# Attention pooling on one core: in TensorE's column-tiled stretch, the sums of the chunk before last are written ahead of the scores of the last one

## The chip, the cores and the metric

The kernel runs on one core of a Trainium2 chip. The metric is the device time of one execution in microseconds (us), lower is better. A core has five engines with instruction streams of their own that wait for each other by semaphores: TensorE (PE in the profile; PEld is its weight load), VectorE (DVE), ScalarE (ACT), GpSimd (POOL) and SyncE (SP), which here only issues DMAs.

## The reference

There are 512 rows (B), each with 200 behaviour vectors (S) of 128 numbers (E) and one candidate vector. Cut to what matters:

```python
W_b, W_c = fc1_w[:E], fc1_w[E:]
h = relu(einsum('bse,eh->bsh', behavior_emb, W_b) + (candidate_emb @ W_c)[:, None, :] + fc1_b)
scores = einsum('bsh,h->bs', h, fc2_w[:, 0]) + fc2_b[0]
attn = softmax(scores, axis=-1)
user_interest = einsum('bse,bs->be', behavior_emb, attn)
x = concatenate([user_interest, candidate_emb], axis=1)
z = relu(x @ mlp1_w + mlp1_b)
logit = (z @ mlp2_w + mlp2_b)[:, 0]
```

All inputs are float32. Nearly all the work is in the first product (512 x 200 vectors times a 128x128 matrix), in the scores and in `user_interest`.

## The kernel before, in words

**Chunks and groups.** The 512 rows are worked on in 32 chunks of 16 rows. A chunk is read twice: as `xt` (transposed, 128 x 4 groups x 800 columns, for the first product) and as `x` (128 x 3200, for the weighted sums). Each goes through four buffers. A group `g` is 800 columns of `xt`, the vectors of 4 rows.

**The first product** is made in three fp32r matmuls: ScalarE casts a group to its high half `xh` (`high_half`, L311), VectorE subtracts that from the original to give the low half `xl` (`low_half`, L440), and TensorE adds `w_hi*xh`, `w_lo*xh` and `w_hi*xl` in PSUM (`products`, L577, L578, L581). A group's result takes two banks; three such pairs (`z_ps0` to `z_ps2`) are used in turn. VectorE reads the results of groups 0 and 2 out (`biased_max`, L450) and ScalarE those of groups 1 and 3 (`biased_relu`, L355), both into `hidden`. So `products` of group 1 of a chunk waits, by `hidden_made` (`banks_read`, L568), until VectorE has read out group 2 of the chunk before it, whose banks it takes.

**Scores.** `score` (L594) multiplies `hidden` with the second layer's column, as 8 small matmuls: four column tiles of the array, one for each group, first with a 32-column weight and 416 columns, then with a 1-column weight and 384 columns. They fill the single bank `s_ps`. VectorE transposes that bank out (`softmax`, step 0, L461) and makes the maximum in five more small steps, up to `exp_bias` (L479). ScalarE makes the exponentials (`exponents`, L319, L321), and GpSimd spreads them into a block matrix (`mask_weights`, L280).

**Weighted sums.** `weighted_sum` (L604) multiplies this block matrix with `x`: 25 small matmuls over the four column tiles, into `u_ps`. Every second chunk the sums are copied out (`copy_pooled4`, L327), transposed by TensorE (`transpose_sums`, L632), and copied again (`copy_pooled_t`, L331), which sets `u_free` for the next even chunk's sums.

**What sets the order.** It is written out by hand: every engine has a function `period(c, q, phase)` that is run once for each chunk `c`. In period `c` TensorE makes the products of the chunk's groups 0 and 1, then in one column-tiled stretch the scores of chunk `c-1` and the weighted sums of chunk `c-2`, then the products of groups 2 and 3. VectorE's period is: `biased_max` of group 0, `low_half` of group 3 and of the next chunk's group 0, the softmax steps of chunk `c-1` (they wait for `scores_done`), `low_half` of the next chunk's group 1, `biased_max` of group 2, `low_half` of the next chunk's group 2. ScalarE's is: `high_half` of the next chunk's group 0, `biased_relu` of group 1, `high_half` (1), in every second period `copy_pooled4`, the exponentials of chunk `c-1`, `high_half` (2), `biased_relu` of group 3, in every second period `copy_pooled_t`, `high_half` (3). SyncE loads `xt` when VectorE has used a buffer up (L235) and `x` when TensorE has (`pooled_done`, L243). The last chunk's scores, the last two chunks' sums and the small network at the end stand behind the loop.

Of the kernel before, what the change touches and what calls it, by code (L numbers as in the profile page):

```python
# [27 lines left out]
X_BUFS = 4  # L28
# [3 lines left out]
PHASE_AT = 1  # L32
# [23 lines left out]
def attention_pooling_kernel(nc, behavior, behavior_t, candidate, first, later, out):  # L56
# [12 lines left out]
    with ExitStack() as ctx:  # L69
# [135 lines left out]
        def loads(c, q):  # L205

            return (c + (X_BUFS - q)) * (16 // X_BUFS)
# [357 lines left out]
        def _(pe):  # L565
# [4 lines left out]
            def products(c, q, g, early):  # L570
                z = z_view(q, g)
                halves = [(0, BANK), (BANK, WIDTH)]
                pe.wait_ge(xh_made, c * GROUPS + (g + 1))
                if not early:
                    banks_read(c, g - Z_BACK[q * GROUPS + g])
                for a, b in halves:
                    nc.tensor.matmul(z[:, a:b], w_hi[:, :], xh[g][:, a:b], start=True, stop=False)  # L577
                    nc.tensor.matmul(z[:, a:b], w_lo[:, :], xh[g][:, a:b], start=False, stop=False)  # L578
                pe.wait_ge(xl_made, c * GROUPS + (g + 1))
                for a, b in halves:  # L580
                    op = nc.tensor.matmul(z[:, a:b], w_hi[:, :], xl[g][:, a:b], start=False, stop=True)  # L581
                op.then_inc(z_done, 1)

            def score(c, buf, early):
                if early:
                    pe.wait_ge(f2_col_made, 2)
                pe.wait_ge(hidden_made, c * HALF + HALF)
                pe.wait_ge(relu_made, c * HALF + HALF)
                if not early:

                    pe.wait_ge(softmax_step, c * SOFTMAX_STEPS - (SOFTMAX_STEPS - 1))
                for rows, t, n in [(Q, 0, RUN), (1, RUN, TILES - RUN)]:
                    for g in range(GROUPS):
                        op = nc.tensor.matmul(  # L594
                            s_ps[g * Q:g * Q + rows, (RUN - n) * Q:RUN * Q].rearrange("p (t s) -> p t s", s=Q),
                            f2_col[:, 0:rows], hidden[buf][:, g, t:t + n, :],
                            start=True, stop=True, tile_position=(0, g * Q))
                op.then_inc(scores_done, 1)

            def sum_tiles(c, q, bank, a, b):  # L600
                buf = q % 2
                for t in range(a, b):
                    g = t % GROUPS
                    op = nc.tensor.matmul(bank[g * Q:(g + 1) * Q, 0:P], weights_by_row[buf][:, t, :],  # L604
                                          x[q][:, t * E:(t + 1) * E], start=buf == 0 and t < GROUPS,
                                          stop=buf == 1 and t >= TILES - GROUPS, tile_position=(0, g * Q))
                return op

            def weighted_sum(c, q):
                pe.wait_ge(x_loaded[q], loads(c, q))  # L610
                pe.wait_ge(masked, c + 1)
                if q % 2 == 0:

                    pe.wait_ge(u_free, c + 1)
                sum_tiles(c, q, u_ps, 0, TILES).then_inc(pooled_done, 1)
# [14 lines left out]
            def transpose_sums(c, bank):  # L630
                pe.wait_ge(pooled4_copied, c + 1)
                nc.tensor.matmul(bank[:, P:P + 2 * ROWS], pooled4[:, :], fold, start=True,  # L632
                                 stop=True).then_inc(pooled_t_done, 2)

            def shift_sums():
                pe.wait_ge(bias_f2_made, 1)
                for g in range(GROUPS):
                    op = nc.tensor.matmul(
                        u_ps[g * Q:(g + 1) * Q, 0:CHUNKS * EACH].rearrange("p (c r) -> p c r", r=EACH), ones[:, 0:Q],
                        bias_f2[:, :].rearrange("p (c r) -> p c r", r=ROWS)[:, :, g * EACH:(g + 1) * EACH],  # L640
                        start=True, stop=True, tile_position=(0, g * Q))
                op.then_inc(shift_done, 1)
# [45 lines left out]
            def transpose_candidates(part):  # L688
                a, b = CAND_PARTS[part]
                pe.wait_ge(cand_loaded[part], 16)  # L690
                for n in range(a, b):
                    op = nc.tensor.transpose(s_ps[:, n * P:(n + 1) * P], cand[:, n, :], ident)
                op.then_inc(cand_t_done, 1)

            def bias_products(part):
                a, b = (n * P for n in CAND_PARTS[part])
                pe.wait_ge(cand_t_copied, part + 1)
                if part > 0:

                    pe.wait_ge(setup_step, 2)  # L700
                nc.tensor.matmul(u_ps[:, a:b], w_c, cand_t[:, a:b], start=True, stop=True).then_inc(bias_done, 1)  # L701
# [10 lines left out]
            def period(c, q, phase):  # L712
                for g in range(GROUPS):
                    products(c, q, g, phase == 0 and g < Z_BUFS)
                    if phase == 0 and g == 0:
                        transpose_candidates(1)
                        bias_products(1)
                    if phase == 0 and g == 2:
                        shift_sums()
                    if g == PHASE_AT and phase >= 1:  # L720
                        score(c - 1, (q + 1) % 2, phase == 1)
                    if g == PHASE_AT and phase >= 2:
                        weighted_sum(c - 2, (q + 2) % X_BUFS)
                    if g == GROUPS - 1 and phase >= 2 and (q - 2) % 2 == 1:
                        transpose_sums(c - 2, u_ps)

            periods(period)(pe)
            score(LAST, LAST % 2, False)
            row_sums(0)
# [64 lines left out]
```

## Time and profile before

| | |
|---|---|
| median of 3 runs | 278.26 us (276.95 to 279.87) |
| the profiled execution's own time | 279.17 us |
| its span, first to last instruction | 277.4 us |
| mean granted TensorE clock | 0.988 |
| TensorE busy | 266.2 us, 96% |
| VectorE busy | 233.5 us, 84% |
| ScalarE busy | 215.4 us, 78% |
| GpSimd busy | 28.8 us, 10% |
| HBM read | 105.70 MB, 381 GB/s over the span |

"Busy" is a share of the span. TensorE's ends are modelled, so that a busy TensorE is not one at its peak; for TensorE the starts of the rows are used below. A row of the timeline merges neighbouring instructions of one line: its start, then the time from the first start to the last end, then how many there are (each fp32 matmul of the scores and of the sums is recorded twice, so 8 instructions are x16 and 25 are x50). In brackets stands how long the engine sat idle before it, and what ended that.

### The profile page before, as it was taken

Reading aid. Unit: us, or ns where it says so; the run is one execution under the profiler, and the core shown is the slowest. Engines: PE = TensorE matmul, PEld = TensorE weight load, DVE = VectorE, ACT = ScalarE, POOL = GpSimd, SP = SyncE. Lnnn points to the kernel's source line nnn. Section 1 sums busy time; section 2 is a strip of 40 time slices with the busy share of each in tenths; the row PEclk is TensorE's granted clock in tenths of the full one; section 3 lists DMA queues with packets and bytes.
Section 4 is the critical chain, followed back from the end, with each engine's and each line's share of the span. In section 5 each row is a group of like instructions: output and inputs, shape, how many; then the busy total and the mean of one; then the engine's idle time right before and its main releaser. Section 6 shows DMA issues by size and latency. Waiting matters only on the chain.

```text
span 277.4 us, 8724 instructions
## 1 busy us (share of the span) xinstructions
PE 266.2 (96%) x2998; PEld 200.2 (72%) x2998; DVE 233.5 (84%) x405; ACT 215.4 (78%) x557; POOL 28.8 (10%) x38
## 2 busy tenths in 40 slices
PE   5969999999999999999999999999999999999895
PEld 4645678777777777887777777787777777777663
DVE  1809999999999999999999999999999999999451
ACT  3466788888889988888888898888888889888412
POOL 2000111111011111111100111111110011111100
PEclk9995999999999999999999999999999999999999
DMA  7999999999999999999999999999999999992000
GB/s 234 438 426 419 433 421 423 423 426 423 428 426 425 432 421 430 425 426 426 430 425 426 430 421 430 425 426 426 430 425 426 430 423 432 421 430 97 0 2 1
DMA packets 10506, 105.84 MB, mean 382 GB/s; under 512 B 1152, under 2 KB 1664, under 8 KB 2432
## 3 DMA queue, kind: packets, MB, share of 16 engines
q1 hardware_dynamic: 10352, 105.39, 90.2%
q10 hardware_dynamic: 144, 0.31, 0.3%
q8 instruction: 6, 0.10, 0.2%
q14 instruction: 4, 0.03, 0.0%
HBM read 105.70 MB, written 0.00 MB: 381 GB/s over the span
## 4 chain that ended last, share of the span: by engine, by line
PE 92%; DVE 2%; ACT 2%; DMA 2%; issue 1%
PE z_ps L577 19%; PE s_ps L594 17%; PE z_ps L581 17%; PE z_ps L578 17%; PE u_ps L604 16%; DMA first_sb<-in_first 2%; PE z_ps L604 1%; DVE xl L440 1%; PE u_ps L701 1%; ACT hidden L355 1%; PE u_ps L632 1%; DVE hidden L450 1%; PE z_ps L673 1%; PE z_ps L667 1%; ACT xh L311 1%
## 5 line engine op out<-in xcount | busy, mean ns | idle before, releaser
L440 DVE TENSOR_TENSOR xl<-xt,xh 128x800 fp32r<-128x800 f32 x128 | 123.9, 988 | 9.4 <-ACT xh L311 8.9
L311 ACT CAST xh<-xt 128x800 fp32r<-128x800 f32 x128 | 108.5, 880 | 1.0 <-DMA xt<-in_behavior_t 0.8
L577 PE MATMUL z_ps<-xh,w_hi 128*128 128x512 f32 (+1 forms) x256 | 95.9, 375 | 3.1 <-ACT xh L311 2.2
L355 ACT ACTIVATE hidden<-z_ps,bias 128x200 f32<-128x200 f32 x256 | 89.2, 442 | 11.7 <-PE z_ps L581 10.5
L578 PE MATMUL z_ps<-xh,w_lo 128*128 128x512 f32 (+1 forms) x256 | 86.7, 353 | 0.0
L450 DVE TENSOR_TENSOR hidden<-z_ps,neg_bias 128x800 f32<-128x800 f32 x64 | 63.2, 988 | 8.7 <-PE z_ps L581 8.3
L581 PE MATMUL z_ps<-xl,w_hi 128*128 128x512 f32 (+1 forms) x256 | 69.6, 354 | 0.0
L577 PEld LDWEIGHTS z_ps<-xh,w_hi 128*128 128x128 f32 x256 | 49.5, 193 | 20.4 <-ACT xh L311 7.4
L604 PEld LDWEIGHTS u_ps<-x,weights_by_row 128*32 128x32 f32 x1500 | 46.5, 110 | 12.3 <-issue 12.3
L578 PEld LDWEIGHTS z_ps<-xh,w_lo 128*128 128x128 f32 x256 | 50.0, 195 | 6.2 <-issue 0.3
L594 PE MATMUL s_ps<-hidden,f_col 128*1 128x384 f32 (+1 forms) x512 | 50.1, 509 | 1.4 <-issue 1.4
L280 POOL TENSOR_TENSOR weights_by_row<-weights,first_sb 128x400 f32<-128x400 f32 x31 | 27.0, 870 | 231.6 <-ACT weights L321 231.6
L604 PE MATMUL u_ps<-x,weights_by_row 128*32 128x128 f32 x1500 | 50.8, 273 | 0.0
L581 PEld LDWEIGHTS z_ps<-xl,w_hi 128*128 128x128 f32 x256 | 42.4, 194 | 0.0
L319 ACT ACTIVATE weights<-scores,exp_bias 128x13 f32<-128x13 f32 x32 | 10.2, 320 | 31.9 <-DVE exp_bias L479 31.8
L594 PEld LDWEIGHTS s_ps<-hidden,f_col 128*1 128x1 f32 (+1 forms) x512 | 11.9, 97 | 25.1 <-issue 24.9
L461 DVE STREAM_TRANSPOSE scores<-s_ps 128x416 f32<-128x416 f32 x32 | 19.5, 610 | 0.5 <-PE s_ps L594 0.4
L479 DVE SCALAR_TENSOR_TENSOR exp_bias<-row_max,shift 128x1 f32<-128x1 f32 x32 | 7.0, 220 | 3.7
L321 ACT ACTIVATE weights<-scores,exp_bias 128x12 f32<-128x12 f32 x32 | 9.7, 303 | 0.0
L469 DVE STREAM_TRANSPOSE part_max_t<-part_max 128x32 f32<-128x32 f32 x32 | 6.8, 211 | 1.4 <-DVE part_max L467 0.3
L327 ACT COPY pooled<-u_ps 128x128 f32<-128x128 f32 x15 | 4.0, 266 | 4.8 <-PE u_ps L604 4.8
L475 DVE STREAM_TRANSPOSE row_max<-row_max_t 128x32 f32<-128x32 f32 x32 | 6.8, 211 | 1.1
(69 smaller groups left out, 83.8 us busy)
## 6 DMA issues: line engine op xcount, KB each, us to landing
x<-in_behavior SPq DMA_DIRECT2D x32, 1600.0 KB, 17.5
xt<-in_behavior_t SPq DMA_DIRECT2D x31, 1600.0 KB, 15.6
xt<-in_behavior_t SPq DMA_DIRECT2D x4, 400.0 KB, 5.5
first_sb<-in_first ACTq DMA_DIRECT2D x1, 307.5 KB, 4.9
later_sb<-in_later SPq DMA_DIRECT2D x1, 258.5 KB, 22.5
cand<-in_candidate SPq DMA_DIRECT2D x1, 192.0 KB, 5.4
cand<-in_candidate SPq DMA_DIRECT2D x1, 64.0 KB, 4.6
out_logit<-logit SPq DMA_DIRECT2D x1, 1.8 KB
```

Source lines behind the costliest of these rows:

```text
L280: nc.gpsimd.tensor_tensor(weights_by_row[buf][:, :, pair_half[buf]], weights[buf][:, :].unsqueeze(2).to_broadcast([P, TILES, ROWS]), row_m ...
L311: nc.scalar.copy(xh[g][:, :], xt[q][:, g, :]).then_inc(xh_made, 1)
L319: nc.scalar.activation(weights[buf][:, 0:RUN], runs[:, 1, :], ACT.Exp, bias=exp_bias[buf][:, :], accum_out=weight_sums[:, c, 0:1]).then_in ...
L355: op = nc.scalar.activation(hidden[q % 2][:, g, :, mine], z[:, :, mine], ACT.Relu, bias=bias[:, bass.ds(c * ROWS + g * EACH + b, 1)])
L440: nc.vector.tensor_tensor(xl[g][:, :], xt[q][:, g, :], xh[g][:, :].bitcast(F32), ALU.subtract).then_inc(xl_made, 1)
L450: nc.vector.tensor_tensor(hidden[q % 2][:, g, :, :].rearrange("p t (b s) -> p t b s", s=PARTS), z, nb.to_broadcast([P, TILES, EACH, PARTS] ...
L461: op = nc.vector.transpose(scores[buf][:, :], s_ps[:, 0:RUN * Q])
L577: nc.tensor.matmul(z[:, a:b], w_hi[:, :], xh[g][:, a:b], start=True, stop=False)
L578: nc.tensor.matmul(z[:, a:b], w_lo[:, :], xh[g][:, a:b], start=False, stop=False)
L581: op = nc.tensor.matmul(z[:, a:b], w_hi[:, :], xl[g][:, a:b], start=False, stop=True)
L594: op = nc.tensor.matmul(s_ps[g * Q:g * Q + rows, (RUN - n) * Q:RUN * Q].rearrange("p (t s) -> p t s", s=Q), f2_col[:, 0:rows], hidden[buf] ...
L604: op = nc.tensor.matmul(bank[g * Q:(g + 1) * Q, 0:P], weights_by_row[buf][:, t, :], x[q][:, t * E:(t + 1) * E], start=buf == 0 and t < GROUPS,
```

## The change

In `period` of TensorE two calls change places: the weighted sums of chunk `c-2` are issued before the scores of chunk `c-1`. Both stay between the products of group 1 and of group 2.

```diff
                     if phase == 0 and g == 2:
                         shift_sums()
+                    if g == PHASE_AT and phase >= 2:
+                        weighted_sum(c - 2, (q + 2) % X_BUFS)
                     if g == PHASE_AT and phase >= 1:
                         score(c - 1, (q + 1) % 2, phase == 1)
-                    if g == PHASE_AT and phase >= 2:
-                        weighted_sum(c - 2, (q + 2) % X_BUFS)
                     if g == GROUPS - 1 and phase >= 2 and (q - 2) % 2 == 1:
```

On TensorE, in a period of the loop, the piece of the difference (rows with + are of the changed kernel; L587 and L591 prepare the scores' waits, L610 that of the sums; L577 and L578 at the end are the products of group 2):

```order
+L610 ISA
+L604 MATMUL u_ps<-x,weights_by_row 32x128 x25
 L587 REGISTER_ALU
 L591 ISA
 L594 MATMUL s_ps<-hidden,f_col 32x416 x4
 L594 MATMUL s_ps<-hidden,f_col 1x384 x4
-L610 ISA
-L604 MATMUL u_ps<-x,weights_by_row 32x128 x25
 L573 REGISTER_ALU
 L577 MATMUL z_ps<-xh,w_hi 128x512
```

The 25 matmuls of the sums, with their wait, have moved from behind the eight of the scores to in front of them. Nothing is added or removed.

On VectorE, in a period of the loop, the instructions from the wait for the scores to the read-out of group 2 (`hidden_made`, for which TensorE's products of the next chunk's group 1 wait), of the kernel before; the changed kernel has the same rows:

```order
L460 ISA [waits scores_done]
L461 STREAM_TRANSPOSE scores<-s_ps 128x416 [waits weights_made]
...
L479 SCALAR_TENSOR_TENSOR exp_bias<-row_max,shift 128x1
L439 REGISTER_ALU
L440 TENSOR_TENSOR xl<-xt,xh 128x800 [waits xh_made]
L450 ISA [waits z_done]
L450 TENSOR_TENSOR hidden<-z_ps,neg_bias 128x800
```

Nothing moved on VectorE: the wait for `scores_done` stands in the same place.

## Rows read from the trace of the kernel before

**Rows 1.** The page: span, busy time of each engine, one line group (mean ns).

```profile
span 277.4 us, 8724 instructions
PE 266.2 (96%) x2998; PEld 200.2 (72%) x2998; DVE 233.5 (84%) x405; ACT 215.4 (78%) x557; POOL 28.8 (10%) x38
...
L604 PE MATMUL u_ps<-x,weights_by_row 128*32 128x128 f32 x1500 | 50.8, 273 | 0.0
```

**Rows 2.** Busy time by stretch; two chunks of the steady part.

```profile
core 0: us, PE busy (x) PEld busy (x) DVE busy (x) ACT busy (x) POOL busy (x), PEclk, DMA share, GB/s
133.10:140.80 7.70, 7.70 (x96) 5.99 (x92) 7.12 (x13) 6.78 (x19) 0.87 (x1) 1.00 1.01 426
140.80:148.50 7.70, 7.70 (x94) 5.75 (x90) 7.15 (x13) 6.38 (x17) 0.87 (x1) 1.00 1.01 426
```

**Rows 3.** Waits: who waited for whom; total us, times, longest.

```profile
ACT xh L311 <- DMA xt<-in_behavior_t: 0.8, 1, 0.8
```

**Rows 4.** Timeline, TensorE, one steady period and the next products.

```profile
139.41 0.40 PE L577 MATMUL z_ps<-xh,w_hi 128*128 128x512 f32 x1
...
140.61 1.55 PE L594 MATMUL s_ps<-hidden,f_col 128*32 128x416 f32 x16
...
141.33 0.10 PEld L594 LDWEIGHTS s_ps<-hidden,f_col 128*1 128x1 f32 x4 [0.24 <-issue]
...
141.66 0.13 PEld L604 LDWEIGHTS u_ps<-x,weights_by_row 128*32 128x32 f32 x4 [0.22 <-issue]
...
141.98 1.69 PE L604 MATMUL u_ps<-x,weights_by_row 128*32 128x128 f32 x50
...
143.60 0.50 PE L577 MATMUL z_ps<-xh,w_hi 128*128 128x512 f32 x1
...
146.98 0.39 PE L577 MATMUL z_ps<-xh,w_hi 128*128 128x512 f32 x1
```

**Rows 5.** Timeline, VectorE and ScalarE, the same period and the next.

```profile
142.46 0.61 DVE L461 STREAM_TRANSPOSE scores<-s_ps 128x416 f32<-128x416 f32 x1
...
144.28 0.98 DVE L440 TENSOR_TENSOR xl<-xt,xh 128x800 fp32r<-128x800 f32 x1
...
145.18 0.98 DVE L450 TENSOR_TENSOR hidden<-z_ps,neg_bias 128x800 f32<-128x800 f32 x1
...
147.30 0.99 DVE L450 TENSOR_TENSOR hidden<-z_ps,neg_bias 128x800 f32<-128x800 f32 x1 [0.21 <-PE z_ps L581]
...
150.17 0.61 DVE L461 STREAM_TRANSPOSE scores<-s_ps 128x416 f32<-128x416 f32 x1
...
155.03 0.20 ACT L331 COPY pooled_t<-u_ps 128x32 f32 x1
```

**Rows 6.** Timeline, VectorE and TensorE, periods 1 and 2.

```profile
27.95 0.62 DVE L461 STREAM_TRANSPOSE scores<-s_ps 128x416 f32<-128x416 f32 x1
...
30.59 0.98 DVE L450 TENSOR_TENSOR hidden<-z_ps,neg_bias 128x800 f32<-128x800 f32 x1
...
31.69 0.19 PEld L577 LDWEIGHTS z_ps<-xh,w_hi 128*128 128x128 f32 x1 [0.66 <-ACT xh L311]
31.72 0.47 PE L577 MATMUL z_ps<-xh,w_hi 128*128 128x512 f32 x1 [0.36 <-DVE hidden L450]
...
32.99 1.55 PE L594 MATMUL s_ps<-hidden,f_col 128*32 128x416 f32 x16
```

**Rows 7.** Timeline, TensorE, VectorE and ScalarE, the last period.

```profile
255.79 1.55 PE L594 MATMUL s_ps<-hidden,f_col 128*32 128x416 f32 x16
...
257.41 0.62 DVE L461 STREAM_TRANSPOSE scores<-s_ps 128x416 f32<-128x416 f32 x1 [0.45 <-PE s_ps L594]
...
261.28 1.38 ACT L355 ACTIVATE hidden<-z_ps,bias 128x200 f32<-128x200 f32 x4 [1.32 <-PE z_ps L581]
...
262.76 1.55 PE L594 MATMUL s_ps<-hidden,f_col 128*32 128x416 f32 x16 [1.38 <-issue]
```

## Prediction

> **What bounds the kernel now.** I read the page first, then the busy time by stretch, the list of waits, and the timeline of one steady period.
>
> The page gives TensorE 96% of the span, against 84% for VectorE and 78% for ScalarE [rows 1]. In the steady part TensorE has no gap at all, at full clock, while VectorE works about 7.1 of 7.7 us [rows 2]. From the scores of the second period to those of the last are 29 periods and 255.79 - 32.99 = 222.80 us [rows 6, 7], so **a period takes 7.683 us**, set by TensorE's own stream. The DMA engines are busy throughout too, at 426 GB/s [rows 2]; two transfers of 1600 KB a period are 3.277 MB, or 7.69 us at that rate. But ScalarE waited for a transfer only once, for 0.8 us [rows 3]: the loads keep up and have no room to go faster for long.
>
> The timeline shows what is nearly late. In the stretch the scores start at 140.61, the sums at 141.98, the next products at 143.60 [rows 4]. VectorE takes the scores up at 142.46 without a wait: it came from other work [rows 5]. Where it did wait for them, at the end, it started 257.41 - 255.79 = 1.62 us after the scores' first matmul [rows 7]; so here they were ready at 140.61 + 1.62 = 142.23, only 0.23 us before VectorE was. Behind the softmax steps VectorE makes a low half (144.28) and reads out group 2 (145.18, done at 146.16) [rows 5]. For that read-out the products of the next chunk's group 1 wait, and they started at 146.98 [rows 4]: **0.82 us to spare**.
>
> **The change, part by part.** Every instruction stays. Three things may cost or gain.
>
> *TensorE's own stretch.* Before, it is 140.61 to 143.60, 2.99 us. From products to tiled matmuls and back there is one passage each way, before and after the change; what is new is the passage from sums to scores. From the sums' first matmul to what follows, no row shows scores. From below, the 50 records span 1.69 us [rows 4] with the last lasting 0.27 [rows 1], and over four column tiles that is a step of 0.11 for each four (12.5 fours in 1.42 us), which makes 1.42 + 0.11 = 1.53. From above, the passage to products takes 143.60 - 141.98 = 1.62 [rows 4], and the whole span is 1.69. I take **1.57**, between 1.53 and 1.62, as the weights of the scores have the same shape as those of the sums but nothing shows them loaded early. The scores until what follows took 1.37 to the sums; to products the same passage may add 0.09. So the stretch, now 2.99, becomes 2.90 to 3.08.
>
> *The sums, earlier by 1.37 us.* They wait for the block matrix, for `x` and for `u_free`. `pooled_done` comes earlier, and so do the load of `x` and ScalarE's first copy of the sums. This hurts nobody: the queue of loads was full anyway. I cost it at nothing; what covers it is the DMA work in flight. If the block matrix came late, the sums would hold the scores up; it depends on the same scores as the read-out below, and is treated there.
>
> *The scores, later by 1.57 us.* This is the term that counts. The scores start 1.57 us later after the same products, so VectorE can take them at 142.23 + 1.57 = 143.80 instead of 142.46: 1.34 us later. Queued behind that wait on VectorE are the six softmax steps, a low half and the read-out of group 2, and the last of these had 0.82 us to spare. So TensorE now waits, in every period. A closed loop takes over, and its length is the new period:
>
> - scores' first matmul to VectorE's transposition, when it waits: 1.62 [rows 7];
> - transposition to the products of the next group 1: 31.72 - 27.95 = 3.77 where TensorE did wait for it [rows 6]. In a steady period the read-out ended 146.16 - 142.46 = 3.70 after the transposition [rows 5], and TensorE began 0.15 after a read-out's end (31.57 to 31.72), 3.85 together. I take 3.80;
> - those products to the first tiled matmul: 32.99 - 31.72 = 1.27 after a wait [rows 6], against 1.20 without (139.41 to 140.61) [rows 4]; I take 1.27, the case that will be there;
> - sums, until the scores' first matmul: 1.57.
>
> Together 1.62 + 3.80 + 1.27 + 1.57 = **8.26 us**, 0.58 over 7.683. TensorE's own work in a period stays near 7.7, so it sits idle for about 0.6 us in each, just before the products of group 1.
>
> On that wait a page bears. TensorE's load of weights for the waiting products started at 31.69 and their matmul at 31.72, both only after the read-out had ended at 31.57 [rows 6]. The Trainium skill (TensorE: Matmul & The Clock Gate, What a matmul computes) has a queue of 64 with a partial reorder window that pulls weight loads ahead of matmuls in flight. By that rule the load would be done during the wait, the products would take 1.20 and the loop 8.19, and the result would be 29 x 0.07 = 2 us lower; the row has the load waiting with its matmul, so the sum goes by the row.
>
> *Both ends.* The first scores that are moved start at 32.99 + 1.57 = 34.56. 29 periods of 8.26 later the last ones in the loop start at 274.1, instead of 255.79: +18.3. Behind them the sums no longer stand. ScalarE's read-out of the last group 3 was at 261.28 after a wait of 1.32 for TensorE [rows 7]; with the sums out of the way TensorE is 1.57 earlier there, ScalarE only 1.32, and the last scores wait for ScalarE: -1.32. The rest is the same work in the same order. Sum: 18.3 - 1.3 = **+17.0 us**. The profiled execution would take 279.17 + 17.0 = 296.2; the median of the runs is 0.9 below it, so I predict **295.3 us**.
>
> *Bounds.* Low: the waits cost nothing beyond the flow without waits, 1.62 - 0.09 (the passage that 1.62 may hold, as 1.62 - 1.53 in the sums) + 3.77 + 1.20 + 1.53 = 8.03, hence 29 x 0.347 + 0.25 = +10.3, 288.6. High: 1.62 + 3.85 + 1.27 + 1.69 = 8.43, hence +21.9, 300.2.
>
> **Rivals.**
>
> *Absorbed (no change).* VectorE has 0.2 us of idle before a read-out of group 0 [rows 5] and 0.6 us in a period [rows 2]; running later by a constant amount would cost nothing if TensorE's waits allowed it. It decides at 0.82 us of lateness at the read-out of group 2. Against it: the lateness is 1.34, the idle time lies behind that read-out, not ahead of it, and TensorE did wait at just this place in period 1 [rows 6]. For it: only if a steady VectorE could take the scores up faster than 1.62. Then only the stretch counts, 30 times from -0.09 to +0.09: 275.6 to 281.0, middle 278.3. Chance 5%.
>
> *Faster.* The changes of weight width within the stretch are one fewer: before, 32 columns (scores), 1 (scores), 32 (sums); after, 32, 32, 1. If TensorE emptied itself at such a change, one emptying a period would go. An emptying is at most the 0.24 or 0.22 us of idle load time there [rows 4], 30 x 0.2 = 6 us, giving 272, and it decides only where the 0.82 us also hold. Against it: the loads of scores and sums follow at 141.33, 141.66 and the sums' matmuls at 141.98, an even step of 0.32 to 0.33 across the change of width [rows 4]; and the loads need 7.69 a period, so a shorter period lasts only while landed tiles lie ahead. The Trainium skill (TensorEngine Tiling (Array Packing), Key Properties) says that changing the tiling mode drains TensorE; the even step shows no drain here, if this is such a change. Chance 3%.
>
> *A longer loop (slower still).* ScalarE's second copy of the sums ends at 155.23, 5.06 after its transposition at 150.17 [rows 5], and the sums of every second period wait for it. With 0.15 for the signal this gives 5.06 + 0.15 + 1.57 + 1.62 = 8.40 in such periods, 0.14 over the forecast: +2, 297.3. The copy had come late by waits on TensorE that may go, so it may not bind. If each released wait on VectorE, ScalarE and GpSimd also adds some 0.1 us that the flowing trace hides, the loop reaches 8.6: 29 x 0.92 + 0.25 = +26.9, about 305. Chance 12%, mostly at its lower end.
>
> *The change does nothing.* The order of TensorE's instructions does change in every period, and no engine's scheduler may put it back; no chance of its own.
>
> **The numbers.** The forecast has 80%, the longer loop 12%, absorbed 5%, faster 3%. The range of 8 in 10 takes the forecast's bounds nearly whole and the lower end of the longer loop: **289 to 301 us**. About 1% (2.8 us) is what a measurement can tell from no change. Slower by over 1%: 92%; within 1%: 5%; faster: 3%.
>
> **What would show it.** In the changed profile: VectorE's transposition (L461) waits for TensorE (L594) in nearly every period, some 29 times for about 0.5 to 0.9 us, where it waited once; TensorE's L577 waits for VectorE's L450 about 29 times for 0.3 to 0.6 us; the distance of the scores is near 8.26, the same in every period rather than uneven; the DMA share of a steady stretch falls to 7.69 / 8.26 = 0.93; TensorE's busy share falls towards 91%. Sums to scores at 1.57 and products to sums at 1.27 check the two terms that I chose. The mechanism is wrong if the transposition does not wait, or if TensorE's gap lies in front of another instruction, say the sums waiting for the block matrix (L604 on L280) or for the copy (L604 on L331), or if the clock falls in the new gaps.

## The result, and the profile after

The changed kernel takes 299.83 us (median of 4 runs, 299.54 to 300.19) where the kernel before takes 278.27. The ratio is 1.0755, with a 95% interval from 1.0721 to 1.0788: slower by 7.5%, inside the range of 289 to 301 us, 4.5 us above the predicted 295.3. The profiled execution took 299.54 us; its span is 297.7.

The page of the changed kernel, against [rows 1]:

```profile
span 297.7 us, 8724 instructions
...
PE 272.9 (92%) x2998; PEld 202.5 (68%) x2998; DVE 234.4 (79%) x405; ACT 210.7 (71%) x557; POOL 28.8 (10%) x38
...
xt<-in_behavior_t SPq DMA_DIRECT2D x31, 1600.0 KB, 8.8
```

VectorE and GpSimd do the same work in nearly the same time; the span has grown by 20.3 us. The list of waits shows where (engine, line, whom it waited for; total us, times, longest):

```profile
DVE scores L461 <- PE s_ps L594: 27.1, 30, 1.7
...
PE z_ps L577 <- DVE hidden L450: 14.5, 31, 0.7
...
ACT xh L311 <- DMA xt<-in_behavior_t: 0.7, 1, 0.7
```

VectorE now waits for the scores 30 times, 0.9 us each, where it waited once [rows 7]. TensorE waits 31 times for VectorE's read-out. No wait for a transfer was added, against [rows 3]. One turn of the loop, from the products of group 1 to the next ones, in the timeline of the changed kernel:

```profile
132.35 0.47 PE L577 MATMUL z_ps<-xh,w_hi 128*128 128x512 f32 x1 [0.35 <-DVE hidden L450]
...
133.62 1.61 PE L604 MATMUL u_ps<-x,weights_by_row 128*32 128x128 f32 x49
...
134.96 0.55 PE L594 MATMUL s_ps<-hidden,f_col 128*32 128x416 f32 x3
135.06 0.27 PE L604 MATMUL u_ps<-x,weights_by_row 128*32 128x128 f32 x1
135.17 1.51 PE L594 MATMUL s_ps<-hidden,f_col 128*32 128x416 f32 x13
...
136.61 0.50 PE L577 MATMUL z_ps<-xh,w_hi 128*128 128x512 f32 x1
...
136.87 0.62 DVE L461 STREAM_TRANSPOSE scores<-s_ps 128x416 f32<-128x416 f32 x1 [0.84 <-PE s_ps L594]
...
139.60 0.98 DVE L450 TENSOR_TENSOR hidden<-z_ps,neg_bias 128x800 f32<-128x800 f32 x1
...
140.70 0.19 PEld L577 LDWEIGHTS z_ps<-xh,w_hi 128*128 128x128 f32 x1 [0.87 <-ACT xh L311]
140.73 0.47 PE L577 MATMUL z_ps<-xh,w_hi 128*128 128x512 f32 x1 [0.56 <-DVE hidden L450]
```

The reader is to see three things. The turn is closed: each of its four links follows on the one before it, and VectorE and TensorE both wait within it. It takes 140.73 - 132.35 = 8.38 us. And TensorE's own stretch, 133.62 to 136.61, is 2.99 us, exactly what it was [rows 4]: the stretch as a whole did not get longer.

The ends, in the timeline of the changed kernel:

```profile
31.70 0.47 PE L577 MATMUL z_ps<-xh,w_hi 128*128 128x512 f32 x1 [0.36 <-DVE hidden L450]
...
34.31 0.55 PE L594 MATMUL s_ps<-hidden,f_col 128*32 128x416 f32 x3
...
36.11 0.62 DVE L461 STREAM_TRANSPOSE scores<-s_ps 128x416 f32<-128x416 f32 x1 [0.93 <-PE s_ps L594]
...
39.88 0.47 PE L577 MATMUL z_ps<-xh,w_hi 128*128 128x512 f32 x1 [0.37 <-DVE hidden L450]
...
277.37 0.55 PE L594 MATMUL s_ps<-hidden,f_col 128*32 128x416 f32 x3
...
281.64 1.35 ACT L355 ACTIVATE hidden<-z_ps,bias 128x200 f32<-128x200 f32 x4
...
283.10 1.55 PE L594 MATMUL s_ps<-hidden,f_col 128*32 128x416 f32 x16 [1.47 <-issue]
```

From the first moved scores to the last are (277.37 - 34.31) / 29 = 8.381 us a period, against 7.683. The whole difference of the spans is thereby accounted for: the start 34.31 - 32.99 = +1.32, 29 periods +20.26, and from the loop's last scores to the end 20.33 instead of 21.61, -1.28; together +20.3 = 297.7 - 277.4.

### The profile page after: what moved, and what is told of

The parts are those of the page before. It is cut to its first block, busy times and chain, and to the rows that moved or that the text cites. A ratio compares the mean times of both kernels' runs of the same rounds, so it can differ in the third digit from the quotient of the medians.

```text
span 297.7 us, 8724 instructions
## 1 busy us (share of the span) xinstructions
PE 272.9 (92%) x2998; PEld 202.5 (68%) x2998; DVE 234.4 (79%) x405; ACT 210.7 (71%) x557; POOL 28.8 (10%) x38
## 4 chain that ended last, share of the span: by engine, by line
PE 53%; DVE 28%; issue 12%; ACT 2%; DMA 2%; DVEq 1%
PE s_ps L594 16%; PE u_ps L604 15%; DVE hidden L450 11%; PE z_ps L577 7%; DVE scores L461 6%; PE z_ps L581 5%; PE z_ps L578 5%; DVE row_max L475 2%; DVE part_max_t L469 2%; DVE part_max L467 2%; DVE row_max_t L471 2%; DVE xl L440 2%; DMA first_sb<-in_first 2%; PE z_ps L604 1%; PE u_ps L701 1%
## 5 line engine op out<-in xcount | busy, mean ns | idle before, releaser
L577 PE MATMUL z_ps<-xh,w_hi 128*128 128x512 f32 (+1 forms) x256 | 98.0, 383 | 16.7 <-DVE hidden L450 14.5
L577 PEld LDWEIGHTS z_ps<-xh,w_hi 128*128 128x128 f32 x256 | 49.4, 193 | 55.5 <-ACT xh L311 27.0
L578 PE MATMUL z_ps<-xh,w_lo 128*128 128x512 f32 (+1 forms) x256 | 86.5, 352 | 0.0
L594 PE MATMUL s_ps<-hidden,f_col 128*1 128x384 f32 (+1 forms) x512 | 55.1, 508 | 1.5 <-issue 1.5
L578 PEld LDWEIGHTS z_ps<-xh,w_lo 128*128 128x128 f32 x256 | 49.8, 194 | 6.2 <-issue 0.3
L604 PE MATMUL u_ps<-x,weights_by_row 128*32 128x128 f32 x1500 | 51.5, 275 | 0.0
L604 PEld LDWEIGHTS u_ps<-x,weights_by_row 128*32 128x32 f32 x1500 | 43.4, 110 | 8.0 <-issue 8.0
L594 PEld LDWEIGHTS s_ps<-hidden,f_col 128*1 128x1 f32 (+1 forms) x512 | 21.5, 97 | 12.6 <-issue 3.3
L467 DVE TENSOR_REDUCE part_max<-scores 128x1 f32<-128x26 f32 x32 | 6.4, 198 | 1.1
```

The source lines that it names most:

```text
L594: op = nc.tensor.matmul(s_ps[g * Q:g * Q + rows, (RUN - n) * Q:RUN * Q].rearrange("p (t s) -> p t s", s=Q), f2_col[:, 0:rows], hidden[buf] ...
```

## The experiments

The theory is the closed loop of the prediction. Its rivals are a cost of the passage from sums to scores in the array itself, a cost in proportion to the work that stands ahead of the scores, and a wait of the sums for the block matrix or for ScalarE's copy.

**How much ahead of the scores.** The sums are cut in two, K matmuls ahead of the scores and the rest behind:

```diff
                     if g == PHASE_AT and phase >= 2:
-                        weighted_sum(c - 2, (q + 2) % X_BUFS)
+                        sums_waits(c - 2); sum_tiles(c - 2, (q + 2) % X_BUFS, u_ps, 0, K)
                     if g == PHASE_AT and phase >= 1:
                         score(c - 1, (q + 1) % 2, phase == 1)
+                    if g == PHASE_AT and phase >= 2:
+                        sum_tiles(c - 2, (q + 2) % X_BUFS, u_ps, K, TILES).then_inc(pooled_done, 1)
```

With K = 12 (e3_split12): 

> The changed kernel with 12 of the 25 sum matmuls ahead of the scores and 13 behind. Loop theory: the loop is 13 x 0.057 = 0.74 shorter than 8.38, 7.64, just under TensorE's 7.68, so 278 to 280 us, and no wait for the read-out. A cost that is in proportion to what stands ahead of the scores gives 278.3 + 21.6 x 12/25 = 288.7. A cost of the passage from sums to scores as such gives the whole 299.8.

Measured: 278.57 us, ratio 0.9989 (0.9961 to 1.0017). Half of the delay costs nothing: the period stays at (255.49 - 32.68) / 29 = 7.683. The cost of the passage and the cost in proportion both fall.

With K = 20 (e4_split20): 

> The same with 20 ahead and 5 behind. Loop theory: the loop is 5 x 0.057 = 0.28 shorter, 8.10, so 29 x (8.10 - 7.68) = 12.1 over before, 290.4 us, with 25 to 31 waits for the read-out of 0.1 to 0.3 us. In proportion: 278.3 + 21.6 x 20/25 = 295.6. The passage as such: 299.8.

Measured: 286.08 us, ratio 1.0269 (1.0236 to 1.0303). It is a closed loop again, but a shorter one than expected. Its turn in the timeline:

```profile
134.50 0.48 PE L577 MATMUL z_ps<-xh,w_hi 128*128 128x512 f32 x1
...
135.77 1.30 PE L604 MATMUL u_ps<-x,weights_by_row 128*32 128x128 f32 x40
...
136.88 1.53 PE L594 MATMUL s_ps<-hidden,f_col 128*32 128x416 f32 x16
...
138.58 0.62 DVE L461 STREAM_TRANSPOSE scores<-s_ps 128x416 f32<-128x416 f32 x1 [0.50 <-PE s_ps L594]
...
141.32 0.98 DVE L450 TENSOR_TENSOR hidden<-z_ps,neg_bias 128x800 f32<-128x800 f32 x1
...
142.45 0.47 PE L577 MATMUL z_ps<-xh,w_hi 128*128 128x512 f32 x1
```

The turn is 142.45 - 134.50 = 7.95 us, and 29 x (7.95 - 7.68) = 7.8 over 278.3 is 286.1, as measured. The read-out ends at 141.32 + 0.98 = 142.30 and the products follow 0.15 later, as in all turns; a gap this short is hardly listed as a wait (3 times in this run, where I had expected 25 or more). I had expected 8.10. From the scores to the transposition it takes 1.70 here and 1.91 in the changed kernel: 0.21 that five matmuls do not explain. The next run looks at the last of them.

With K = 24 (e7_split24): 

> The changed kernel with 24 sum matmuls ahead of the scores and only the last one behind. With 20 ahead the turn was 7.95. Loop theory with the time for each four: 4 more matmuls are 0.23, so 8.18, and 278.3 + 29 x 0.50 = 292.8 us. The 25th matmul alone then costs 0.20 a turn, as it sits in one column tile and holds that tile's scores up. If each matmul costs the same 0.057, 24 ahead give 299.8 - 1.7 = 298.1.

Measured: 292.91 us, ratio 1.0512 (1.0478 to 1.0547), as expected. The period is (270.31 - 33.57) / 29 = 8.16. A turn in the timeline:

```profile
138.44 1.52 PE L604 MATMUL u_ps<-x,weights_by_row 128*32 128x128 f32 x48
139.77 1.53 PE L594 MATMUL s_ps<-hidden,f_col 128*32 128x416 f32 x16
141.11 0.38 PE L604 MATMUL u_ps<-x,weights_by_row 128*32 128x128 f32 x2
...
141.47 0.62 DVE L461 STREAM_TRANSPOSE scores<-s_ps 128x416 f32<-128x416 f32 x1 [0.71 <-PE s_ps L594]
```

One matmul less ahead of the scores is worth 6.9 us. 24 fill six rounds over the four column tiles; the 25th stands alone in one. In the changed kernel three scores begin at 134.96 beside it, and the other thirteen follow from 135.17. The scores' last matmul ends at 135.17 + 1.51 = 136.68, which is 1.72 after their first began, against 1.53 here. From the first scores to the transposition it is 1.70 without the lone matmul and 1.91 with it, though the scores start at the same distance (1.33 and 1.34). What stands behind the scores is not the cause: from their last matmul's end to the transposition it is 0.17 (141.30 to 141.47) and 0.19 (136.68 to 136.87).

**VectorE's loop written out.** The changed kernel, and only on VectorE the hardware loop replaced by 32 periods with constants:

```diff
-            periods(period)(dve)
+            for c in range(CHUNKS):
+                period(c, c % X_BUFS, LAST if c == LAST else min(c, FIRST))
```

On the changed kernel (e5_vector_unrolled): 

> The changed kernel with VectorE's loop over periods written out, so that its waits and addresses are constants; all else as it is. In the changed kernel's trace a turn of the loop takes 8.18 us in period 2, which stands ahead of the hardware loop (31.70 to 39.88), and 8.38 within it (132.35 to 140.73): 0.11 more from the scores to the transposition and 0.09 more in the softmax steps, just where VectorE's queue has instructions of its own. If these are the cause, 28 periods lose 0.20 each: 294.2 us. If it is crowding by other engines that builds up only later, 299.8 stays.

Measured: 293.52 us, ratio 1.0531 (1.0493 to 1.0570). The transpositions are 142.15 - 133.96 = 8.19 apart:

```profile
133.96 0.62 DVE L461 STREAM_TRANSPOSE scores<-s_ps 128x416 f32<-128x416 f32 x1 [0.74 <-PE s_ps L595]
...
142.15 0.62 DVE L461 STREAM_TRANSPOSE scores<-s_ps 128x416 f32<-128x416 f32 x1 [0.83 <-PE s_ps L595]
```

On the kernel before (e6_before_vector_unrolled): 

> The same on the kernel before, as control. There VectorE is not waited for, so its queue's instructions cost nothing: 277 to 279 us. If writing the loop out were worth something by itself, this would show it.

Measured: 279.15 us, ratio 0.9999 (0.9974 to 1.0025). So 6.3 us of the change's cost come from writing VectorE's loop as a hardware loop, and the two places where a turn in that loop is longer than in period 2, by 0.11 and 0.09, are those where VectorE's queue has register and wait instructions of its own. They cost nothing that shows in the kernel before, and count once the wait is in the loop. The chain of waits of the changed kernel names them, between the scores and the transposition, and ahead of `exp_bias` (start, us, what); the trace of e5_vector_unrolled has none at either place:

```profile
145.14 0.05 DVEq L460
...
145.24 0.63 DVE scores L461
...
146.84 0.05 DVEq L479
```

**Taking the link out.** On VectorE the read-out of group 2 is put ahead of the low half of the next group 1:

```diff
+                biased_max(c, q, 2, phase < 2)
                 if phase != LAST:
                     low_half(c + 1, nq, 1)
-                biased_max(c, q, 2, phase < 2)
```

On the changed kernel (e1_readout_first): 

> The changed kernel, and on VectorE the read-out of group 2 ahead of the low half of the next chunk's group 1. Theory (a closed loop scores, softmax steps, read-out, products of group 1, sums, scores): the link from the transposition to the read-out loses one low half, 0.90 us, so the loop of 8.38 becomes 7.48 and drops below TensorE's own 7.68: 278 to 280 us, and TensorE's L577 no longer waits for L450. Rival (the passage from sums to scores costs TensorE itself some 0.7 us a period): nothing changes there, 299 to 300 us. Rival (the sums wait for the block matrix or for ScalarE's copy): these keep their distance to the scores, 299 us.

Measured: 290.00 us, ratio 1.0409 (1.0380 to 1.0439). TensorE waits for the read-out only once in the whole run, so the link is out, and 9.8 us come back; but I had expected 20. The control (e2_before_readout_first): 

> The kernel before with the same exchange on VectorE alone, as the control: TensorE's stream sets the period in either order, 277 to 279 us by every theory. Were it faster by over 2 us, the exchange would be worth something by itself and e1_readout_first would have to be read against it.

Measured: 284.83 us, ratio 1.0221 (1.0184 to 1.0259). The control came out otherwise than expected, too: the exchange itself costs the kernel before 5 to 6 us, so something else had come in. The waits and the timeline of e1_readout_first:

```profile
PE u_ps L604 <- ACT pooled_t L331: 7.2, 14, 0.6
...
PE z_ps L577 <- DVE hidden L450: 0.6, 1, 0.6
```

```profile
142.18 0.99 DVE L450 TENSOR_TENSOR hidden<-z_ps,neg_bias 128x800 f32<-128x800 f32 x1
...
143.09 2.56 DVE L440 TENSOR_TENSOR xl<-xt,xh 128x800 fp32r<-128x800 f32 x2
...
143.16 1.64 POOL L280 TENSOR_TENSOR weights_by_row<-weights,first_sb 128x400 f32<-128x400 f32 x1 [6.37 <-ACT weights L321]
...
145.00 0.19 ACT L331 COPY pooled_t<-u_ps 128x32 f32 x1
...
145.33 1.58 PE L604 MATMUL u_ps<-x,weights_by_row 128*32 128x128 f32 x49 [0.57 <-ACT pooled_t L331]
```

GpSimd spreads the weights into the block matrix just when VectorE makes a low half. Two low halves, 1.88 to 1.90 us elsewhere, take 2.56, and GpSimd's operation 1.64 instead of 0.87. VectorE's stream grows from some 7.4 to 7.93. In the old order the read-out, whose input is in PSUM, stands there, and neither is longer (0.98 at 139.60 and 0.87 at 139.78 in the changed kernel). The row of two low halves hides which of them pays; narrower windows of the timeline show them one by one:

```profile
143.09 0.98 DVE L440 TENSOR_TENSOR xl<-xt,xh 128x800 fp32r<-128x800 f32 x1
...
143.99 1.66 DVE L440 TENSOR_TENSOR xl<-xt,xh 128x800 fp32r<-128x800 f32 x1
```

They take turns. The first low half, begun 0.07 before GpSimd's operation, keeps its 0.98 and ends at 144.07. GpSimd's ends 0.73 after that, at 144.80. The second low half ends 0.85 after that, at 145.65. The Trainium skill (SBUF — State Buffer, Who interferes with whom) says that a VectorE instruction with two SBUF inputs contends with a GpSimd instruction that reads SBUF, for ports that are locked exclusively, and that the loser blocks for the whole instruction. The trace agrees on who contends and on the turns.

In every second period the sums wait for ScalarE's copy, the longer loop of my third rival: a turn of 148.55 - 140.27 = 8.28 us between transpositions, with 7.93 in the period before it.

Three runs (2 executions each) with GpSimd's operation cut to 2 of 25 columns tell the two apart. They leave out the spreading of the other 23 columns, which stay zero, so the sums are incomplete while TensorE does the same work:

```diff
-                    weights_by_row[buf][:, :, pair_half[buf]],
-                    weights[buf][:, :].unsqueeze(2).to_broadcast([P, TILES, ROWS]),
-                    row_mask.unsqueeze(1).to_broadcast([P, TILES, ROWS]), ALU.mult).then_inc(masked, 1)
+                    weights_by_row[buf][:, 0:2, pair_half[buf]],
+                    weights[buf][:, 0:2].unsqueeze(2).to_broadcast([P, 2, ROWS]),
+                    row_mask.unsqueeze(1).to_broadcast([P, 2, ROWS]), ALU.mult).then_inc(masked, 1)
```

On the changed kernel (e9_small_mask): 

> The changed kernel, with GpSimd spreading only 2 of the 25 columns of weights (the rest of the block matrix stays zero, so the pooled vectors are not complete). Control for the next two: the loop does not pass through the block matrix, and GpSimd's operation falls beside a read-out from PSUM, not beside a low half: 299 to 300 us. If the sums' wait for the block matrix were in the loop: under 290.

Measured: 299.63 us, ratio 1.0715 (1.0633 to 1.0798). The block matrix is not in the loop.

On e1_readout_first (e10_readout_first_small_mask): 

> e1_readout_first with the same small spreading. In e1_readout_first the low half and the spreading of the block matrix ran at the same time and took 1.66 and 1.61 us instead of 0.99 and 0.87, which made VectorE's own stream about 8 us a period. Theory: without that overlap VectorE's stream is back at 7.4; what is left is the turn through ScalarE's second copy of the sums in every second period (8.28 there) and 7.48 in the others, 15.76 for two, so 278.3 + 29 x 0.20 = 284 us. If the two did not slow each other down, 290 stays.

Measured: 284.66 us, ratio 1.0180 (1.0077 to 1.0283). Two periods now take 146.95 - 131.06 = 15.89, near the 15.76 expected: 7.60, and 8.29 in the one with the copy. The copy and the sums that wait for it, and what GpSimd's small operation takes beside a low half:

```profile
141.56 1.01 POOL L280 TENSOR_TENSOR weights_by_row<-weights,first_sb 128x32 f32<-128x32 f32 x1 [6.67 <-ACT weights L321]
...
143.39 0.19 ACT L331 COPY pooled_t<-u_ps 128x32 f32 x1
143.73 1.58 PE L604 MATMUL u_ps<-x,weights_by_row 128*32 128x128 f32 x49 [0.45 <-ACT pooled_t L331]
```

On e2_before_readout_first (e11_before_readout_first_small_mask): 

> e2_before_readout_first with the small spreading. Sums stand behind the scores, so no loop passes through the copy of the sums: TensorE's own stream sets the period again, 277 to 280 us. If the read-out's place and not the overlap made e2_before_readout_first slow, 284.8 stays.

Measured: 276.25 us, ratio 0.9879 (0.9805 to 0.9954), a little under what was expected. In its timeline the small operation takes 0.24 where no low half runs, and the period is (252.31 - 29.54) / 29 = 7.68, TensorE's own:

```profile
29.54 1.55 PE L594 MATMUL s_ps<-hidden,f_col 128*32 128x416 f32 x16 [0.38 <-issue]
...
142.14 0.24 POOL L280 TENSOR_TENSOR weights_by_row<-weights,first_sb 128x32 f32<-128x32 f32 x1 [7.33 <-ACT weights L321]
...
252.31 1.55 PE L594 MATMUL s_ps<-hidden,f_col 128*32 128x416 f32 x16
```

So the period is back, and the rest of the difference lies ahead of 29.54, where the kernel before is 3.45 us later (32.99). Part of that is the clock of the profiled executions: from 20 to 27 us the granted clock was 0.51 in the kernel before and 0.86 in this run. How much is the edit's stays open. The three runs together: the overlap made the exchange slow, and the changed order has a second loop, through the copy, just under the first.

**A version that is faster than both.** The end of the changed kernel was 1.28 us shorter, since no sums stood ahead of the last read-out. In the kernel before, the sums of chunk 29 alone can be moved into TensorE's idle time before the last scores:

```diff
-                    if g == PHASE_AT and phase >= 2:
+                    if g == (GROUPS - 1 if phase == LAST else PHASE_AT) and phase >= 2:
                         weighted_sum(c - 2, (q + 2) % X_BUFS)
...
             row_sums(0)
+            transpose_sums(LAST - 2, u_ps)
```

(ScalarE's two copies of that pair stand behind its last read-out.) e8_before_last_sums_later: 

> The kernel before, with one thing moved in the last period alone: the weighted sums of chunk 29 stand behind the products of group 3 instead of behind the scores (their copies on ScalarE and their transposition move with them). Theory: in both kernels TensorE sat idle for 1.38 to 1.47 us before the last scores, waiting for ScalarE's read-out of group 3, and the changed kernel was 1.28 us shorter from the loop's last scores to the end because no sums stood ahead of that read-out. Here the sums fill that idle time: about 1.0 to 1.3 us less than before, ratio 0.996. Rival: the late transposition and copies hold up the network at the end, and nothing or less is gained.

Measured: 277.12 us against 278.89, ratio 0.9943 (0.9921 to 0.9965), a small gain whose interval lies clear of 1. The timeline of the last period (line numbers are two higher here):

```profile
255.07 1.55 PE L596 MATMUL s_ps<-hidden,f_col 128*32 128x416 f32 x16
...
258.94 1.72 PE L606 MATMUL u_ps<-x,weights_by_row 128*32 128x128 f32 x50
...
259.16 1.36 ACT L355 ACTIVATE hidden<-z_ps,bias 128x200 f32<-128x200 f32 x4
...
260.62 1.55 PE L596 MATMUL s_ps<-hidden,f_col 128*32 128x416 f32 x16
```

The sums run beside ScalarE's read-out, and the last scores follow the loop's last ones by 5.55 us instead of 6.97 [rows 7]. From those to the end of the span (275.5) it is 20.43 us, against 21.61: 1.18 less, as expected. The rest of the measured 1.8 is not explained by this edit: in the profiled executions the scores of period 2 already start at 32.27 instead of 32.99, and up to there the two kernels are the same program.

## Why the prediction was right, and which terms were off

**The mechanism held.** The scores came later, VectorE waited for them, the read-out behind that wait came later than its 0.82 us to spare, and TensorE waited for it in every period. The split runs show that it begins to cost between 12 matmuls ahead of the scores (nothing) and 20 (a loop), and taking the read-out forward took TensorE's wait away. The block matrix has no share (e9_small_mask). The passage from sums to scores has one, though not in TensorE's own stretch, where I looked for it: the lone 25th matmul lets the scores finish 0.21 later in each turn, and I had no term for that.

**The four terms of the loop,** predicted and measured:

| link | predicted | measured |
|---|---|---|
| products of group 1 to the first sums | 1.27 | 1.27 (132.35 to 133.62) |
| sums to the first scores | 1.57 | 1.34 (to 134.96) |
| scores to the transposition | 1.62 | 1.91 (to 136.87) |
| transposition to the products of group 1 | 3.80 | 3.86 (to 140.73) |
| together | 8.26 | 8.38 |

Two terms were mis-sized, by -0.23 and +0.29, and their errors nearly cancelled; that the total came out close is in part luck. The step "sums, until the scores' first matmul" took the sums as finished before the scores begin; in fact three scores start while the 25th matmul is still alone in its column tile. What that gave, the step "scores' first matmul to VectorE's transposition" took back: its 1.62 came from a period behind the hardware loop and without a lone matmul. The lone matmul adds 0.21 (1.70 to 1.91), and VectorE's queue 0.11 (1.80 in period 2, 36.11 - 34.31, to 1.91 in the loop). For the step "transposition to products" I took the middle between 3.77, read ahead of the hardware loop, and 3.85, read within it; the one within it was right, with the same 0.09 of queue instructions.

The 0.12 a period is 3.5 us of the 4.5. The start was 0.25 less than predicted and the end 0.04 more. The last 1.2 us lie between profiled executions and medians: the one of before took 0.9 more than its median, the changed one 0.3 less.

**The end** was predicted at -1.32 and measured at -1.28, by the named step: ScalarE's last read-out no longer waits and follows its exponentials. **The longer loop** through the copy was real but did not bind: predicted at 8.40, it showed at 8.20 to 8.30 in every second period as soon as the first loop was shortened (e1_readout_first, e10_readout_first_small_mask), just under the 8.38 of the first. **Weight loads.** The sum was right to go by the row: in the changed kernel the load starts at 140.70 and its matmul at 140.73, after the read-out, and products to sums took 1.27, not 1.20. The Trainium skill (TensorE: Matmul & The Clock Gate, Architectural detail: the array is 16× 32×32, not 1× 128×128) states its rule for weight loads ahead of matmuls in flight. Here the wait for the read-out (L568) is an instruction of its own ahead of the load, so these rows do not test the rule, and it could not be used for this wait as I had used it. **Tiling mode.** The stretch stayed at 2.99 with one change of weight width fewer, so no drain at that change is seen. The Trainium skill (TensorEngine Tiling (Array Packing), Key Properties) says that a change of tiling mode drains TensorE; whether a change of width is one, no run here shows.

**One sign was wrong.** I expected the DMA share to fall to 0.93. The rate fell, the share did not:

```profile
133.00:141.38 8.38, 7.82 (x92) 5.84 (x91) 7.16 (x13) 6.36 (x18) 0.87 (x1) 1.00 0.99 390
141.38:149.76 8.38, 8.03 (x94) 6.06 (x93) 7.15 (x13) 6.37 (x18) 0.87 (x1) 1.00 0.99 396
```

3.277 MB in 8.38 us are 391 GB/s, at a share of 0.99; a transfer of `xt` landed after 8.8 us instead of 15.6 before. So the share of 1.01 in [rows 2] did not by itself show that the loads had reached their limit, as I had read it.

## What to carry to other kernels

Before two pieces of work on the busiest engine change places, follow the one that comes later to the engine that waits for it, and add up what is queued behind that wait until it comes back to the first engine: if the sum around the circle is longer than the present period, the circle is the new period. Take each link from a place where the wait really occurs and inside the same kind of loop, since queue instructions that cost nothing on an engine that runs ahead can count within a closed loop (0.20 us a turn here). A small operation may also sit where it does because its neighbour there leaves it alone; look at what runs beside it on the other engines before moving either.

## What the runs showed of the hardware that was not expected

- TensorE starts the next small matmuls in some column tiles while another tile is still at the last stream: scores at 134.96, a sum at 135.06. With 25 matmuls over four tiles the lone one delays the end of the scores behind it, by 0.21 us a turn: moving it behind the scores was worth 6.9 us over the kernel (299.83 against 292.91).
- A VectorE operation with two SBUF inputs and a GpSimd operation take turns. A low half kept its 0.98 us, GpSimd's spreading beside it took 1.64 instead of 0.87, and the low half behind them 1.66. A GpSimd operation of 128x32 took 1.01 beside a low half and 0.24 alone.
- VectorE's register and wait instructions within a hardware loop cost 0.2 us a turn when they stand behind a wait in a closed loop (8.38 to 8.19 with the loop written out, 6.3 us in all), and nothing that shows in the kernel before (ratio 0.9999).
- The DMA engines' busy share hardly moved, from 1.01 to 0.99, when their rate fell from 426 to between 390 and 396 GB/s.
